# Four graph layers in a software pipeline: how destination logits reach all partitions, the PSUM banks, the opening and the order

## The reference

```
0: deg * (h Wi' + b) + adj (h Wj')
1: softmax over j of mask(leaky(e_src[i] + e_dst[j])) times Wh      (Wh = h W, width 256)
2: the same with width 128 (hh = h W2), and hh itself as the other 128 columns
3: attention of 8 heads of 32, masked by adj, then the output projection
```

## Time and profile before

| | |
|---|---|
| median of 3 runs | 1323.29 us |
| profiled execution | 1325.42 us, its span 1323.6 us |
| TensorE | busy 1271.1 us (96%), its weight loads 1160.1 us |
| VectorE | busy 1119.2 us (85%) |
| ScalarE | busy 1032.0 us (78%) |
| GpSimd | busy 918.4 us (69%) |
| transfers | 8.7% of 16 engines' span, 29 GB/s |
| granted clock | 0.995 over the span |

### The profile page before, as it was taken

One profiled execution on the slowest core, in us unless ns is written; L12 is line 12 of the kernel. 1 busy time (PEld: TensorE's weight loads), 2 busy tenths in 40 slices (PEclk: granted clock), 3 DMA queues, 4 the chain that ended last, 5 costly groups with the idle time before them and its releaser, 6 DMA issues. The chain is left out here.

```text
span 1323.6 us, 42593 instructions
## 1 busy us (share of the span) xinstructions
PE 1271.1 (96%) x12433; PEld 1160.1 (88%) x12433; DVE 1119.2 (85%) x5726; ACT 1032.0 (78%) x3905; POOL 918.4 (69%) x1225
## 2 busy tenths in 40 slices
PE   2899999999999999999999999999999999999985
PEld 1589999999999999999999999999999999999874
DVE  4688988888888898898888888889888888888863
ACT  0368888878888888887888888888888788888875
POOL 2467777777777777777777777777777777776653
PEclk9899999999999999999999999999999999999999
DMA  3100110010011011001001101101100110100000
GB/s 106 31 18 18 34 34 26 26 33 30 22 34 34 18 34 34 26 26 33 26 26 33 34 18 34 33 21 31 34 26 26 34 34 18 34 26 10 19 17 25
DMA packets 38900, 38.98 MB, mean 29 GB/s; under 512 B 3088, under 2 KB 38672, under 8 KB 38672
## 3 DMA queue, kind: packets, MB, share of 16 engines
q1 hardware_dynamic: 38672, 36.26, 8.7%
HBM read 19.47 MB, written 16.78 MB: 27 GB/s over the span
## 5 line engine op out<-in xcount | busy, mean ns | idle before, releaser
L677 ACT ACTIVATE exps<-masked,nmax 128x128 f32<-128x128 f32 x1024 | 399.3, 409 | 2.2 <-POOL probs L300 2.2
L300 POOL TENSOR_TENSOR probs<-exps,rsum 128x512 f32<-128x512 f32 x256 | 266.9, 1043 | 156.2 <-DVE rsum L506 156.2
L272 POOL TENSOR_TENSOR rstd<-veps,power 128x2 f32<-128x2 f32 x256 | 178.4, 697 | 205.1 <-DVE veps L411 204.7
L280 POOL TENSOR_SCALAR y<-x,nm,rstd 128x256 f32<-128x256 f32 x512 | 281.0, 560 | 22.9 <-issue 21.5
L498 DVE CUSTOM_DVE_ANT_0 masked<-bank,mask 128x128 f32<-128x128 f32 x1024 | 227.4, 283 | 2.0 <-PE bank L869 2.0
L677 ACT ACTIVATION_READ_ACCUMULATOR exps<-masked,nmax 128x1 f32 x1024 | 212.4, 207 | 0.0
L767 PE MATMUL bank<-w_hi,ht_hi 128*128 128x512 f32 (+1 forms) x512 | 195.2, 381 | 5.4 <-DVE ht_lo L440 4.9
L395 DVE BATCH_NORM_STATS2 stats<-x 128x6 f32<-128x256 f32 x512 | 190.2, 413 | 2.3
L768 PE MATMUL bank<-w_lo,ht_hi 128*128 128x512 f32 (+1 forms) x512 | 175.5, 343 | 0.0
L769 PE MATMUL bank<-w_hi,ht_lo 128*128 128x512 f32 (+1 forms) x512 | 174.9, 342 | 0.0
L663 ACT ACTIVATE at<-bank 128x256 f32<-128x256 f32 x128 | 49.3, 385 | 145.6 <-PE bank L828 145.4
(11 more groups left out here) (120 smaller groups left out, 3706.4 us busy)
## 6 DMA issues: line engine op xcount, KB each, us to landing
x<-in_x SPq DMA_DIRECT2D x64, 256.0 KB, 2.8
out<-x SPq DMA_DIRECT2D x64, 256.0 KB, 2.1
probs<-in_w0t SPq DMA_DIRECT2D x1, 512.0 KB, 4.8
w_sb<-in_w SPq DMA_DIRECT2D x1, 256.0 KB, 5.5
probs<-in_w1t SPq DMA_DIRECT2D x1, 256.0 KB, 5.5
exps<-in_wqt SPq DMA_DIRECT2D x1, 256.0 KB, 5.2
exps<-in_wkt SPq DMA_DIRECT2D x1, 256.0 KB, 5.5
exps<-in_wvt SPq DMA_DIRECT2D x1, 256.0 KB, 5.5
```

The source lines that it names most:

```text
L272: pool.tensor_tensor(rstd[i][:, b], veps[i][:, b], power[:], ALU.pow).then_inc(S[f"rstd{i}"], 1)
L280: last = pool.tensor_scalar(y[i][:, b, g], src[:, bx, g], nm[i][:, s, g:g + 1], rstd[i][:, s, g:g + 1], ALU.add, ALU.mult)
L300: pool.tensor_tensor(probs3[:, p % BUFFERS["probs3"], j], exps3[:, p % BUFFERS["exps3"], j], rsum3[:, s, j].unsqueeze(2).to_broadcast([P, ...
L677: last = act.activation(exps3[:, b, j, i], masked3[:, p % BUFFERS["masked3"], j, i], ACT.Exp, bias=nmax3[:, s, j, i:i + 1], scale=-1.0, ac ...
```

## The change

1. `spread_dst` is no longer called. SP writes the column of destination logits of a pair (128 partitions x 2 graphs, 4 bytes each) to a row in DRAM (`write_row`) and reads that row back into all 128 partitions (`spread_row`, 128 KB) into a new SBUF buffer db, two deep. ACT reads db instead of PSUM.
2. The sloped logits of both layers stand in bank 7, which nothing else uses: tasks zz2 and zz1 take it in turn, freed by nmax2 and nmax1. `sum_logits` gets a `bank_free` for it. The other tasks share banks 0 to 6 in a new assignment.
3. The opening: the weights come in on two queues (SP, ACT) with a semaphore for each group; each use waits for its own. The hi part of w0 is made by ACT, its lo part by DVE, and the parts of wq, wk, wv and wo by GpSimd, in the step of its first rstd2. PE multiplies the attention vectors into the weights ahead of the first aggregation, and DVE splits w1 ahead of the first h1t_lo. ACT executes a first Exp on a small buffer. Some unused constants go.
4. Lags and order: the way of a pair is one step longer (store at lag 6), and the order of every engine's step is new.

```diff
 LAG = {
-  "load": -4, "store": 5, "m1": 0, "pt3": 5, "v_mm": 4, "ot_mm": 5, "wh1_mm": 1, "wh0_mm": 1, "s0": 0, "h2t": 2, "d1": 1, "h0t": -1, "h3t": 3,
-  "pt2": 4, "x4_mm": 5, "hh_mm": 2, "kt_mm": 3, "e1t": 1, "d2": 2, "qt_mm": 3, "x2_mm": 1, "pt1": 4, "scores": 3, "m0": -1, "e2t": 2, "pt0": 4,
-  "h1t": 0, "x3_mm": 2, ...
+  "store": 6, "load": -4, "row_in1": 0, "row_out2": 1, "row_in2": 1, "row_out1": -1, "ot_mm": 6, "x2_mm": 2, "h3t": 4, "wh1_mm": 1, "pt1": 5,
+  "wh0_mm": 1, "s0": 0, "h0t": -1, "x4_mm": 6, "qt_mm": 4, "kt_mm": 4, "e2t": 3, "h2t": 2, "pt0": 5, "x3_mm": 3, "m0": -1, "pt3": 5, "pt2": 5,
+  "scores": 4, "hh_mm": 2, "m1": -1, "v_mm": 4, "h1t": 0, "e1t": 1, ...
 }
 BANKS = {
-    "d1": (5, "d1", ('nmax1',)),
-    "d2": (7, "d2", ('nmax2',)),
+    "zz2": (7, "z2", ('nmax2',)),
+    "zz1": (7, "z1", ('nmax1',)),
 ...
+        db = [None] + [sb(f"db{i}", [P, 2, G * P]) for i in (1, 2)]
+        rows = [None] + [nc.dram_tensor(f"rows{i}", [2, G, P], F32).ap() for i in (1, 2)]
 # SP
+            def write_row(i, src, buffer, ready, col, p):
+                b, bs = p % 2, p % BUFFERS[buffer]
+                passed(sp, ready, p)
+                sp.dma_start(rows[i][b].rearrange("g n -> n g"), src[:, bs, :, col], allow_slow_non_contiguous=True).then_inc(row_out[i][b], 16)
+
+            def spread_row(i, p):
+                b = p % 2
+                sp.wait_ge(row_out[i][b], (p // 2 + 1) * 16)
+                passed(sp, f"z{i}", p, 2)
+                sp.dma_start(db[i][:, b], rows[i][b].rearrange("g n -> (g n)").partition_broadcast(P)).then_inc(row_in[i][b], 16)
+
             def step(t):          # store, load, row_in1, row_out2, row_in2, row_out1
 # ACT
             def sum_logits(i, src, buffer, col, p):
-                passed(act, f"d{i}", p)
-                for g in range(G):
-                    last = act.activation(bank_of(f"d{i}")[:, (G + g) * P:(G + g + 1) * P], bank_of(f"d{i}")[:, g * P:(g + 1) * P], ACT.Prelu, ...)
+                act.wait_ge(row_in[i][p % 2], (p // 2 + 1) * 16)
+                bank_free(act, f"zz{i}", p)
+                for g in range(G):
+                    last = act.activation(bank_of(f"zz{i}")[:, g * P:(g + 1) * P], db[i][:, p % 2, g * P:(g + 1) * P], ACT.Prelu, ...)
 # POOL, once, ahead of its first rstd2
+            def split_w3():
+                pool.wait_ge(wk_in, 32)  # and wq_in, wv_in, wo_in
+                for w, (hi, lo) in ((wk_sb, wk_r), (wq_sb, wq_r), (wv_sb, wv_r), (wo_sb, wo_r)):
+                    pool.tensor_copy(hi[:], w).then_inc(w3_high, 1)
+                for i, (w, (hi, lo)) in enumerate(...):
+                    pool.wait_ge(w3_high, i + 1)
+                    pool.tensor_tensor(lo[:], w, hi[:].bitcast(F32), ALU.subtract).then_inc(w3_split, 1)
```

More of the change, by code:

```diff
@@ L29 @@
 LAG = {
[9 rows of a table removed]
[10 rows of a table added]
 }
 BANKS = {
[L43 to L47, removed]
+    "ot": (5, "ot_mm", ('ot_lo',)),
+    "x2b": (4, "x2_mm", ('x2',)),
+    "h3t": (6, "h3t", ('h3t_lo',)),
+    "wh1": (2, "wh1_mm", ('wh1',)),
+    "pt1": (1, "pt1", ('p3t_1',)),
     "wh0": (0, "wh0_mm", ('wh0',)),
     "x1b": (2, "s0", ('x1',)),
-    "h2t": (7, "h2t", ('ht2',)),
-    "d1": (5, "d1", ('nmax1',)),
[L52 to L58, removed]
-    "d2": (7, "d2", ('nmax2',)),
[L60 to L68, removed]
-    "pt0": (2, "pt0", ('p3t_0',)),
-    "h1t": (5, "h1t", ('h1t_lo',)),
-    "x3b": (7, "x3_mm", ('x3',)),
+    "h0t": (4, "h0t", ('h0t_lo',)),
+    "x4b": (5, "x4_mm", ('x4',)),
+    "qt": (3, "qt_mm", ('qt',)),
+    "kt": (0, "kt_mm", ('kt',)),
+    "at2": (6, "e2t", ('at2',)),
+    "h2t": (4, "h2t", ('ht2',)),
+    "pt0": (2, "pt0", ('p3t_0',)),
+    "x3b": (6, "x3_mm", ('x3',)),
+    "m0": (3, "m0", ('mj_lo0', 't0_0')),
+    "pt3": (5, "pt3", ('p3t_3',)),
+    "pt2": (1, "pt2", ('p3t_2',)),
+    "sc0": (6, "scores", ('nmax3_0',)),
+    "sc1": (2, "scores", ('nmax3_1',)),
+    "sc2": (4, "scores", ('nmax3_2',)),
+    "sc3": (0, "scores", ('nmax3_3',)),
+    "hh": (5, "hh_mm", ('hh',)),
+    "m1": (1, "m1", ('mj_lo1', 't0_1')),
+    "v": (3, "v_mm", ('v',)),
+    "h1t": (2, "h1t", ('h1t_lo',)),
+    "at1": (6, "e1t", ('at1',)),
+    "zz2": (7, "z2", ('nmax2',)),
+    "zz1": (7, "z1", ('nmax1',)),
 }
@@ L142, in gnn_kernel @@
         at = [None] + [sb(f"at{i}", [P, BUFFERS[f"at{i}"], G, P]) for i in (1, 2)]
+        db = [None] + [sb(f"db{i}", [P, 2, G * P]) for i in (1, 2)]
+        rows = [None] + [nc.dram_tensor(f"rows{i}", [2, G, P], F32).ap() for i in (1, 2)]
+        row_out = [None] + [[sem(f"row{i}_out{b}") for b in range(2)] for i in (1, 2)]
+        row_in = [None] + [[sem(f"row{i}_in{b}") for b in range(2)] for i in (1, 2)]
         kt = sb("kt", [P, BUFFERS["kt"], DC, G * P])
@@ L233, in _ @@
+                if due(t, "row_in2"):
+                    spread_row(2, t - LAG["row_in2"])
+                if due(t, "row_out1"):
+                    write_row(1, wh, "wh", last_of("wh0", "wh1"), D + 1, t - LAG["row_out1"])
             load(0)
+            sp.dma_start(adj_i[:], adj).then_inc(adj_in, 16)
+            sp.dma_start(w0_sb, w0t.rearrange("(c p) o -> p c o", p=P)).then_inc(w0_in, 16)
+            sp.dma_start(deg_b[:], bias0.partition_broadcast(P)).then_inc(b0_in, 16)
             load(1)
[L235 to L248, removed]
@@ L376, in _ @@
-            for c in range(DC):
-                dve.tensor_copy(w1_sb[:, c, D:D + 2], bank[1][:, 2 * c:2 * c + 2])
-                dve.tensor_copy(w2_sb[:, c, F1:F1 + 2], bank[2][:, 2 * c:2 * c + 2])
-            dve.scalar_tensor_tensor(c3[:], bank[3][:, 0:D], nan_row[:], c3[:], ALU.add, ALU.add).then_inc(c_dve, 1)
-            dve.wait_ge(c_dve, 8)
-            dve.tensor_copy(w1_r[0][:], w1_sb[:]).then_inc(c_dve, 1)
-            dve.wait_ge(c_dve, 9)
-            dve.tensor_tensor(w1_r[1][:], w1_sb[:], w1_r[0][:].bitcast(F32), ALU.subtract).then_inc(c_dve, 1)
+            dve.wait_ge(adjacency, 3)
@@ new lines, in split_w1 @@
+            def split_w1():
+                dve.wait_ge(products, 1)
+                dve.wait_ge(adjacency, 7)
+                for c in range(DC):
+                    last = dve.tensor_copy(w1_sb[:, c, D:D + 2], preparation[:, P + 4 * c:P + 4 * c + 2])
+                last.then_inc(w1_whole, 1)
+                for c in range(DC):
+                    dve.tensor_copy(w2_sb[:, c, F1:F1 + 2], preparation[:, P + 4 * c + 2:P + 4 * c + 4])
+                dve.scalar_tensor_tensor(c3[:], preparation[:, D:2 * D], nan_row[:], c3[:], ALU.add, ALU.add).then_inc(c3_made, 1)
+                dve.wait_ge(w1_whole, 1)
+                dve.tensor_copy(w1_r[0][:], w1_sb[:]).then_inc(w1_high, 1)
+                dve.wait_ge(w1_high, 1)
+                dve.tensor_tensor(w1_r[1][:], w1_sb[:], w1_r[0][:].bitcast(F32), ALU.subtract).then_inc(w1_split, 1)
@@ L526, in step @@
                     stats_of(2, x2, t - LAG["stats2"])
+                if due(t, "h3t_lo"):
+                    relu_transposed_low(3, ht3_r, last_of("kt_mm", "qt_mm", "v_mm"), t - LAG["h3t_lo"])
+                if due(t, "mv2"):
+                    mean_and_variance(2, t - LAG["mv2"])
+                if due(t, "nmax2"):
+                    mask_logits(2, mask2, t - LAG["nmax2"])
+                if due(t, "veps2"):
+                    shifted_variance(2, t - LAG["veps2"])
+                if due(t, "x1"):
+                    sum_x1(t - LAG["x1"])
@@ new lines, in step @@
+                if due(t, "mv1"):
+                    mean_and_variance(1, t - LAG["mv1"])
+                if due(t, "qt"):
+                    add_bias("qt", qt, bq_sb, float(DH) ** -0.5, t - LAG["qt"])
+                if due(t, "stats0"):
+                    stats_of(0, x0, t - LAG["stats0"])
+                if due(t, "rsum3_2"):
+                    inverse_sum3(2, t - LAG["rsum3_2"])
+                if due(t, "x4"):
+                    sum_x4(t - LAG["x4"])
+                if due(t, "kt"):
+                    add_bias("kt", kt, bk_sb, 1.0, t - LAG["kt"])
@@ new lines, in step @@
+                if due(t, "x3"):
+                    sum_x3(t - LAG["x3"])
+                if due(t, "veps1"):
+                    shifted_variance(1, t - LAG["veps1"])
+                if due(t, "stats3"):
+                    stats_of(3, x3, t - LAG["stats3"])
+                if due(t, "nmax1"):
+                    mask_logits(1, mask, t - LAG["nmax1"])
+                if due(t, "mv3"):
+                    mean_and_variance(3, t - LAG["mv3"])
+                if due(t, "t0_0"):
+                    add_own(0, t - LAG["t0_0"])
@@ L711, in step @@
                     high_ot(t - LAG["ot_hi"])
+                if due(t, "exp3_0"):
+                    exps3_of(0, t - LAG["exp3_0"])
+                if due(t, "h3t_hi"):
+                    relu_transposed_high(3, ht3_r, last_of("kt_mm", "qt_mm", "v_mm"), t - LAG["h3t_hi"])
                 if due(t, "wh1"):
                     copy_projection1(1, t - LAG["wh1"])
```

(46 more changed lines are left out.)

378 lines of the change are left out of this document (179 added, 199 removed), and 15 rows, old and new, of the table LAG.

## The result

The changed kernel takes 2242.94 us (2240.39 to 2245.71, 4 runs) where the kernel before takes 1324.44 (1323.06 to 1326.27, 4 runs): 1.693 times as long, 95% interval 1.691 to 1.695. The forecast was 1300 us, with a range of 1279 to 1332.

The account below looks back on a forecast made before the run. PE was taken as the bound: 64 steps of 19.07 us make 1220.5 us, and opening, part-filled steps and emptying add 79.5 us, giving 1300 us. The range was 1279 to 1332 us.

Parts of the forecast that it names:

- What bounds the kernel, and what PE saves: PE sets the pace at 19.51 us a pair; dropping four transposes of logits saves 0.44, leaving 19.07 us.
- Edit 1, the round trip R: SP's column write to DRAM and row read back take 5.3 us, bounds 4.2 to 9.8.
- Edit 1, who waits: ACT in z1 repeats in round trip plus 11.4 us, 16.7 in all, under 19.07; layer 2's trip is hidden.
- rival B: DVE's order binds: late load of x delays x4 and x3, PE loses 0.35 us a step, 1322 us; chance 0.17.
- Rival A: The round trip is long and ACT waits in z1; at 9 us, step 20.4 us, 1385 us; chance 0.13.
- The load of x (rival B): Behind SP's wait for wh, lands 1 + 2.8 us after it; priced at nothing, at most 0.35 us a step.
- Edits 2 to 4: Bank for sloped logits, no own price; opening, PE starts at 12 us; one more lag; outside 64 steps 79.5 us.
- the four terms 4.7, 5, 2 and 8 us: Outside the steps: PE's weight products 4.7, POOL's splits 5, DVE's w1 split 2, extra lag and exposed trips 8 us.

Follow-up runs that it names:

- e3: Changed kernel with each column write made one piece of 1 KB from partition 0 (numbers written are not the destination logits): 1290.57 us.
- e7: Changed kernel with the column's 256 pieces of 4 bytes written 512 bytes apart in DRAM, another row read back: 1302.1 us.
- e13: Changed kernel with the load of x (lag -5) issued ahead of SP's wait for wh and of layer 1's column: 2135.80 us.
- e14: Changed kernel with only layer 2 on the row transfers, db of layer 1 constant: 1702.43 us.
- e1: Changed kernel without row transfers, db filled once with 0.5, destination logits left out: 1288.21 us, ratio 0.9729 to the kernel before.

## Why the prediction was wrong, by its steps

- **What bounds the kernel, and what PE saves.** Right: 19.07 us a pair forecast, 19.09 without the transfers; transposes 0.44 forecast, 0.38 measured.
- **Edit 1, the round trip R: the step that failed.** I put it at 5.3 us, between 4.2 and 9.8. It is 9.4 + 4.2 = 13.6 us in layer 1 and about 12 in layer 2, outside both bounds. They came from rows whose writes go to DRAM in pieces of 1 KB (the store) and whose small transfers go into SBUF (the load of bq): neither writes small pieces to DRAM. With one piece instead, the trip is back within my bounds, 1.1 + 3.2 us, and the kernel takes 1290.6 us with all its waits (e3); with the same 256 pieces 512 bytes apart, 1.9 + 3.1 us, it takes 1302.1 (e7). I had written that no row shows what 256 elements of 4 bytes add, and then closed the range as if it did. That sentence was an open end, and the range had to have one.
- **Edit 1, who waits.** I priced ACT's z1 alone, R + 11.4 us; with R = 13.6 that is 25.0, and the step is 34.2. The trip of layer 2 I called hidden at "some 7 us" of cover, true for 5.3 and not for 12. Three more cycles run through PE, DVE and SP, and I had looked at the first alone (rival B): the load behind the column (e13 takes it away and gains 1.9 us a pair), both trips one behind the other (25.8 of e13's 32.5 us), and bank 0 from wh to kt (in the chain of e14, not tested alone). Rival A was the right mechanism with a step of 20.4 us; its chance of 0.13 was too low for a cost without a row.
- **The load of x (rival B).** I saw its place behind the wait for wh, but gave it 2.8 us to land and the whole mechanism at most 0.35 us a step. Issued 1 us behind the column in the same queue, it took 10.5, and PE's wait for x4 alone is 372.3 us, 5.8 a step: a slow transfer is paid by those behind it. With a fast column DVE waits 34.3 us for x in all (e3), and PE loses nothing.
- **Edits 2 to 4.** Right or better: seven banks are enough, PE's first transposes of y are at 14.06 us (forecast 12), and all outside the steps is 64 to 65 us in e1 and e3 (forecast 79.5). With 14.06 in place of 12 the four terms 4.7, 5, 2 and 8 us have 2.5 us left between them instead of 19.7; the runs do not tell which was too high. Of the last one, the exposed trips cost little when the column is fast: e3, with trips, ends 2.4 us after e1.

## What to carry to other kernels

A small transfer was priced here by the shape of its pieces on the side that it writes, not by its bytes: a column of 4-byte numbers written side by side to DRAM took 7 to 8 us for 0.5 or 1 KB, and turning it first into runs of 128 bytes took it to 1.6. Where the trace has no row of the same kind, leave the range open at that end, and follow every queue and buffer behind the wait around to where it closes, not only the engine that waits. A cheap run with the same waits and one large piece (e3) would have told it at once.

## What the runs showed of the hardware

- Small writes to DRAM took longer the more of them were neighbours: 256 of 4 bytes took 7.8 us side by side and 1.9 us at 512 bytes apart; 128 of 4 bytes 7.2 us side by side and 2.1 us in groups of 16 with 512 bytes from group to group; into SBUF 256 took 2.4 us.
- The load of x (256 KB) lands in 2.8 us behind a fast column and in 10.5 us behind a slow one, though in the changed kernel the queue's packets take 19.9% of the time of the 16 transfer engines. By that share they look idle, and yet what stands behind waits.
